# Attention exponentials split by PSUM bank, and value loads moved ahead of query and key loads

## The reference

```python
scores = jnp.einsum('bhqd,bhkd->bhqk', q, k) * SCALE
scores = jnp.where(causal, scores, -jnp.inf)
probs = jax.nn.softmax(scores, axis=-1)
out = jnp.einsum('bhqk,bhkd->bhqd', probs, v)
```

## Time and profile before

| | |
|---|---|
| median of 3 runs | 702.61 us (697.5 to 704.05) |
| the profiled execution | 697.29 us, span 695.6 us |
| mean granted TensorE clock | 0.932 of full speed |
| busy share of the span | PE 87%, PEld 73%, DVE 71%, ACT 51%, POOL 48% |
| chain that ended last, by engine | PE 42%, DVE 5%, POOL 5%, issue 5%, DMA 3%, ACT 3% |
| costliest attention line on ACT | L370, 48 calls, 49.1 us |

### The profile page before, as it was taken

The page is one execution under the profiler, slowest core; times in us unless marked ns, Lnnn a source line. Parts: engine busy times, 40 slices in busy tenths (PEclk is TensorE's granted clock), DMA queues, the critical chain, the costliest instruction groups (busy, mean ns, idle before and its releaser), DMA issues.

```text
span 695.6 us, 11909 instructions
## 1 busy us (share of the span) xinstructions
PE 603.9 (87%) x4100; PEld 504.4 (73%) x4100; DVE 497.2 (71%) x1066; ACT 352.9 (51%) x685; POOL 334.5 (48%) x322
## 2 busy tenths in 40 slices
PE   3787998998989789899998616999999999999992
PEld 2566887787876545466564416999999999999991
DVE  6887687788698857578883632778787888788740
ACT  4674563663553233353534213565666666656551
POOL 1065424324240014222543673446786868686776
PEclk9897999999999999899998655999999999999997
DMA  8411315775349756765745106233626262521224
GB/s 266 135 32 39 113 31 151 257 191 150 94 93 234 164 122 159 198 148 147 200 131 169 39 14 228 70 101 80 168 33 179 27 179 31 172 31 14 26 33 45
DMA packets 63317, 81.65 MB, mean 117 GB/s; under 512 B 10296, under 2 KB 47939, under 8 KB 63257
## 3 DMA queue, kind: packets, MB, share of 16 engines
q1 hardware_dynamic: 53928, 72.85, 37.4%
q0 software_dynamic: 9216, 7.81, 7.8%
q10 hardware_dynamic: 112, 0.23, 0.1%
HBM read 48.27 MB, written 34.36 MB: 119 GB/s over the span
## 4 chain that ended last, share of the span: by engine, by line
PE 42%; DVE 5%; POOL 5%; issue 5%; DMA 3%; ACT 3%; POOLq 0%; SPq 0%; ACTq 0%; DVEq 0%
PE l_scores L101 13%; PE l_turned L1899 7%; PE l_out L1899 3%; PE l_shared L1899 3%; PE l_turned L340 2%; POOL out L1603 2%; PE l_out L360 2%; PE l_turned L324 2%; POOL disp L1572 2%; PE l_scores L1833 2%; ACT l_area L370 2%; PE l_shared L1775 2%; PE l_scores L1856 1%; PE l_scores L265 1%; DMA l_hi<-vd 1%
## 5 line engine op out<-in xcount | busy, mean ns | idle before, releaser
L2088 DVE SCALAR_TENSOR_TENSOR w_v<-w_th,l_scores 128x324 f32<-128x324 f32 x128 | 62.2, 490 | 56.3 <-ACT w_th L1690 53.9
L1690 ACT ACTIVATE w_th<-l_scores 128x324 f32<-128x324 f32 x128 | 56.5, 441 | 84.0 <-PE l_scores L101 82.7
L1590 POOL TENSOR_TENSOR l_lo<-w_v,l_hi 128x324 fp32r<-128x324 f32 x64 | 59.0, 922 | 74.9 <-ACT l_hi L1696 74.7
L370 ACT ACTIVATE l_area<-l_turned 128x1024 f32<-128x1024 f32 x48 | 49.1, 1023 | 80.5 <-PE l_turned L340 77.4
L101 PE MATMUL l_scores<-l_hi,w_w1h 128*128 128x324 f32 x256 | 81.3, 318 | 2.3 <-DVE l_lo L2080 1.2
L1603 POOL DMA_INDIRECT out<-l_area,w_to x48 | 76.3, 1591 | 12.1 <-issue 9.7
L101 PE MATMUL l_scores<-l_lo,w_w1h 128*128 128x324 f32 x256 | 80.7, 315 | 0.0
L101 PE MATMUL l_scores<-l_hi,w_w1l 128*128 128x324 f32 x256 | 80.6, 315 | 0.0
L294 DVE TENSOR_REDUCE l_nm<-l_scores 128x4 f32<-128x1024 f32 (+1 forms) x45 | 54.7, 1216 | 22.0 <-PE l_scores L280 21.8
L1696 ACT ACTIVATE l_hi<-w_v 128x324 fp32r<-128x324 f32 x128 | 59.9, 472 | 12.4 <-DVE w_v L2088 11.8
L2062 DVE TENSOR_TENSOR w_w2l<-w_s,w_w2h 128x256 fp32r<-128x256 f32 x56 | 60.2, 1075 | 1.9
(11 more groups left out here) (459 smaller groups left out, 1704.1 us busy)
## 6 DMA issues: line engine op xcount, KB each, us to landing
w_s<-in_L_ffn_w SPq DMA_DIRECT2D x14, 1024.0 KB, 7.6
disp<-c_blank SPq DMA_DIRECT2D x8, 658.1 KB
l_lo<-kd SPq DMA_DIRECT2D x26, 200.0 KB
l_hi<-qd SPq DMA_DIRECT2D x26, 192.0 KB
w_rows<-disp SPq DMA_DIRECT2D x7, 658.1 KB
kd<-l_qkh SPq DMA_DIRECT2D x16, 256.0 KB, 4.7
vd<-l_area SPq DMA_DIRECT2D x4, 1024.0 KB, 6.5
qd<-l_qkh SPq DMA_DIRECT2D x16, 256.0 KB, 4.2
```

What stands on the lines that cost most here:

```text
L370: act.activation(lead.pr[n % 3][:, :], lead.tbank[:, :], ACT.Exp, scale=SCALE).then_inc(A["exp"], 1)
L1590: pool.tensor_tensor(hl[:, g % 3, half(1)], v[:, n % 4, :], hh[:, g % 3, half(1)].bitcast(F32), ALU.subtract)\
L1690: act.activation(th[:, n % 2, :], hb[n % 2][:, 0:HALF], ACT.Tanh, scale=0.5).then_inc(F["th"], 1)
L2088: dve.scalar_tensor_tensor(v[:, n % 4, :], th[:, n % 2, :], 1.0, hb[n % 2][:, 0:HALF], ALU.add, ALU.mult).then_inc(F["v"], 1)
```

## The change

There are two edits.

One: the exponentials of a step are made by two ACT calls of 512 columns, one per PSUM bank, and each counts on its own. So `turned` and `turned_mask` take the bank e as an argument, `st` and `exp` count twice per step, and the waits on them are doubled. In the second block PE now issues: mask of bank 0, products of bank 0, the `mask` matmuls of step t + 6, mask of bank 1, products of bank 1. In the first block: mask 0, products 0, mask 1, products 1.

Two: in SP's queue `load_values` stands right after `store_maxima`, ahead of `lay`, the query stores and the weight loads of that group.

```diff
-    ge(sp, A["st"], 3 * (g - ITEMS + 1))
+    ge(sp, A["st"], 6 * (g - ITEMS + 1))
...
+def turned_mask(pe, A, c, lead, n, e):
+
+    ge(pe, A["exp"], 2 * n + e - 1)
     if n == 0:
         pe.wait_ge(A["nm"], LEAD)
...
+    bank = lead.tbank[:, e * 4 * P:(e + 1) * 4 * P]
+    m = 4 if n % 3 == 2 else 2
...
+def turned(pe, A, lead, n, e):
 
     g, s = divmod(n, 3)
-    if s == 0:
+    if s == 0 and e == 0:
         pe.wait_ge(A[f"m_in{g % 2}"], 32 * (g // 2 + 1))
...
-    for p, e in heads(s):
-        rows = slice(64 * e, 64 * e + 3 * HD + 2)
...
+    rows = slice(64 * e, 64 * e + 3 * HD + 2)
...
+    for p in range(4):
+        if s == 2 or p // 2 == s:
+            at = e * 4 * P + (p if s == 2 else p % 2) * w
+            mm = pe.matmul(lead.tbank[:, at:at + w], kx[rows, p, key], q[rows, p, tok], start=False, stop=True,
+                           skip_group_check=True)
     mm.then_inc(A["st"], 1)
...
-    pe.wait_ge(A["exp"], n + 1)
+    pe.wait_ge(A["exp"], 2 * n + 2)
...
-    act.wait_ge(A["st"], n + 1)
     ge(act, A["pv"], n - 2)
-    act.activation(lead.pr[n % 3][:, :], lead.tbank[:, :], ACT.Exp, scale=SCALE).then_inc(A["exp"], 1)
+    for e in range(2):
+        act.wait_ge(A["st"], 2 * n + e + 1)
+        bank = slice(e * 4 * P, (e + 1) * 4 * P)
+        act.activation(lead.pr[n % 3][:, bank], lead.tbank[:, bank], ACT.Exp, scale=SCALE).then_inc(A["exp"], 1)
...
                     store_maxima(sp, A, lead, md, g)
+                    if g % 2 == 0 and g >= 4:
+                        load_values(sp, A, M, lead, vd, g // 2)
                     if 5 < g + 3 < GR:
                         lay(sp, A, M, lead, qd, kd, g + 3)
...
-                    if g % 2 == 0 and g >= 4:
-                        load_values(sp, A, M, lead, vd, g // 2)
...
                     if t < NS:
-                        turned_mask(pe, A, c, lead, t)
+                        turned_mask(pe, A, c, lead, t, 0)
+                        turned(pe, A, lead, t, 0)
                     if u < NS:
                         mask(pe, A, c, lead, u)
                     if t < NS:
-                        turned(pe, A, lead, t)
+                        turned_mask(pe, A, c, lead, t, 1)
+                        turned(pe, A, lead, t, 1)
```

More of the change, by code:

```diff
@@ L307, in turn_maxima @@
     dve.transpose(lead.mt[g % 2][:, :], mx[:, :, :].rearrange("q n c -> q (n c)").bitcast(F32)).then_inc(A["mx"], 1)
[L310 to L317, removed]
+def turned_mask(pe, A, c, lead, n, e):
+    ge(pe, A["exp"], 2 * n + e - 1)
     if n == 0:
         pe.wait_ge(A["nm"], LEAD)
[L320 to L328, removed]
+    bank = lead.tbank[:, e * 4 * P:(e + 1) * 4 * P]
+    m = 4 if n % 3 == 2 else 2
+    out = bank.rearrange("k (p q) -> k p q", p=m)[:, :, 0:P]
+    pe.matmul(out, c["mask"][:, :], c["identb"][:, :].unsqueeze(1).to_broadcast([P, m, P]),
+              start=True, stop=False, skip_group_check=True)
+def turned(pe, A, lead, n, e):
     g, s = divmod(n, 3)
-    if s == 0:
+    if s == 0 and e == 0:
         pe.wait_ge(A[f"m_in{g % 2}"], 32 * (g // 2 + 1))
     q, kx = lead.q3[g % ITEMS], lead.k3[g % ITEMS]
-    for p, e in heads(s):
-        rows = slice(64 * e, 64 * e + 3 * HD + 2)
[L336 to L341, removed]
+    rows = slice(64 * e, 64 * e + 3 * HD + 2)
+    tok = slice(P, L) if s == 2 else slice(0, L)
+    key = slice(P, L) if s == 2 else slice(0, P)
+    w = P if s == 2 else L
+    for p in range(4):
[3 more added lines that the diff above has]
+                           skip_group_check=True)
     mm.then_inc(A["st"], 1)
@@ L990, in step @@
                 def step(t):
-                    turned_mask(pe, A, c, lead, t)
-                    turned(pe, A, lead, t)
+                    for e in range(2):
+                        turned_mask(pe, A, c, lead, t, e)
+                        turned(pe, A, lead, t, e)
                 turn_x(0)
```

## The result

| kernel | median | executions | ratio to the kernel before, 95% interval |
|---|---|---|---|
| before | 701.80 us | 697.5 to 704.05, 5 | |
| changed | 749.93 us | 749.39 to 763.2, 5 | 1.0706 [1.0628, 1.0785] |

The change makes the kernel 7% slower. I had forecast slower, at 712 us, with 722 as the upper end. The five executions of the changed kernel lie at 749.4 to 749.9 us (three) and at 761.9 to 763.2 us (two), and the profiled one, 763.2 us, is one of the slower two; where sums are made, experiment 2 stands in for it, which has the same order on PE and whose profiled execution (750.65 us, span 748.9) agrees with the medians.

What follows compares the result with a forecast made beforehand. PE was taken to bound the attention, with small waits for ACT. Terms +23.8 - 5.0 - 2.3 - 3.4 - 1.0 = +12.1 on the profiled 697.29 us gave 709.4, predicted as 712 for a median of new runs; range 696 to 722.

Steps and rivals of the forecast that it cites:

- +.50 and +.70 per step: PE's attention steps: lost pairs and two more switches lengthen 256-column steps .76 to 1.26 us, 128-column steps 1.12 to 1.82.
- 20.4 us for steps 4 to 39: PE's added work in the attention to 361 us: 24 x .50 + 12 x .70 = 20.4 us.
- -3.4: About seven us at clock .51 after PE's stall for values, counted at full clock without the stall: -3.4 us.
- Steps 0 to 3, 40 to 45 and the rest: PE's added work: 2.2 us in 0 to 3, 0 in 40 to 43, 1.2 in 44 and 45, last two steps 0.
- +7.3 us hidden: ACT's two exponential calls instead of one: +.15 us per step, 7.3 over 48, hidden in ACT's idle time.
- The 5.0 us of waits: PE's waits for exponentials in the attention, 3.5 us shown, taken as 5.0 us gained.
- -2.3: PE's wait for the values of batch 2, until 282.86 us, goes when their load is issued earlier: -2.3 us.
- The 1.0 us for DVE: One wait of PE for DVE in the attention, absorbed by slower PE steps: -1.0 us.
- 1: PE's attention steps 4 to 39: PE's queue hides the added work, only gains stay, 686 to 691 us; chance .10.
- 2: PE's attention steps: only the loss of pairs is paid, 11.6 against 11.7 us gained, 697 to 703 us; chance .24.
- 3: Values' load: the 2.3 us reappear at group 5's maxima and the clock falls anyway; 715, up to 720; chance .12.
- rival 4: Products in one row half load their weights in the open, 9 us more, 718 to 724 us; chance .09.

Runs made afterwards that it cites:

- experiment 2: Kernel before with only PE's new order of masks and products; one exponential call per step, values' load not moved: 752.86 us, ratio 1.0698.
- experiment 9: Kernel before with odd heads' products in `turned` reading the even heads' rows, so no pairs and no added switch: 723.03 us, ratio 1.0298.
- experiment 5: Kernel before with pairs kept, but half of them ahead of the `mask` pair and half behind it: 718.08 us, ratio 1.0239.
- experiment 10: Changed kernel with the products of `turned` taken over all 128 rows: 707.13 us, ratio 1.0080.
- experiment 4: Kernel before with all products of bank 0 issued ahead of those of bank 1, in one place: 699.38 us, ratio 0.9969.
- experiment 3: Kernel before with two counted exponential calls after the last product, each turned mask waiting for one; pairs kept: 700.64 us, ratio 1.0005.
- experiment 1: Kernel before with only the `load_values` line moved as in the change: 699.97 us, ratio 0.9950.
- experiment 7: Kernel before with two counted exponential calls, pairs kept in one place, and the values' load moved ahead: 696.20 us, ratio 0.9942.
- experiment 11: Changed kernel with the second mask of a step waiting for the first bank's exponentials of the same step: 775.62 us, ratio 1.1068.
- experiment 12: Changed kernel with each mask of the turned bank issued four times in a row: 774.31 us.

## Why the prediction was wrong

**The step that failed: every step was priced at full clock.** I wrote +.50 and +.70 per step and summed 20.4 us for steps 4 to 39 from rows at full clock, and I gave the clock one term, -3.4, as something that PE loses after a stall and gets back without one. No rival had a long stretch of lower clock in which PE is busy. The runs show that term: 21 to 24 us in steps 4 to 39 (experiment 2, an estimate), against a miss of 750 - 712 = 38. The clock stays at the half level for 17 to 31 us at a time while PE is shown busy, when the products of a step share one half of the rows (experiment 9, once) or are cut by more switches (experiment 5); with both, as in the change, the loss is larger than the two together (18 + 22 us against 52 in experiment 2); with products over all rows the low stretches are 14 us and less and nearly all of the loss is gone (experiment 10).

**The prices of a step were right.** 1.30 and 1.84 us against 1.26 and 1.82, and the estimate of some 20 us of added work in experiment 2 stands beside the sum of 20.4. The reason I gave was half right: the pairs are lost since masks stand between the halves, not because one half's products are issued in a row (experiment 4).

**Steps 0 to 3, 40 to 45 and the rest.** In experiment 2 its span is 748.9 - 695.6 = 53.3 longer, 43.5 of it in steps 4 to 39; 3.6 lie ahead of them, where I had 2.2, and 6.2 behind, where I had 1.2. Behind them the half level lasts 64.8 us (418.3 to 428.6 and 432.0 to 486.6) against 51.2 before (371.8 to 378.6 and 388.8 to 433.2), so there, too, the clock has a part.

**Edit one on ACT.** +7.3 us hidden: right (8.0 us, 57.1 busy against 49.1, with ACT idle for 134.1). The 5.0 us of waits did go, but experiment 3 shows them to be worth nothing alone: 1.0005 [0.9965, 1.0045].

**Edit two.** Of -2.3 - 3.4, alone 0 to 7 us came (experiment 1), which holds the sum of 5.7 but does not tell the two terms apart. No run shows the clock's 3.4: the profiled execution of experiment 1, the slowest of its ten, has 107.0 us at .94 for steps 4 to 39, no better than before. In the changed kernel the 2.3 us wait is gone, 2.1 us of waits for maxima are new, and that place, 263 to 294, is at .51. The 1.0 us for DVE went as costed.

**The rivals.** 1 and 2: every switch in the new steps is paid. 3: its mechanism is real, waits for maxima of 1.8 us in experiment 1, 3.8 in experiment 7 and 2.1 in the changed kernel, but small. 4: products in one half follow after .12 (experiment 9), so their loads are hidden. That speaks against the rule on weight loads that rival 4 took from the Trainium skill, for products of one half too.

**What stays open.** Whether it is the logits that bring the clock down and the output projection that brings it back, as the places in experiment 2 suggest; and whether it is the empty rows or the short gaps at a switch that keep it down, since lost pairs and switches each go with long low stretches. The Trainium skill, "TensorE: Matmul & The Clock Gate", section "A second HAM failure mode: psum-queue depth-cycling", tells of a kernel whose clock swings between its two levels because PE idles briefly and often between groups of matmuls. Experiment 5 fits it (.83 with more switches). Experiment 11 does not bear it out: with pauses of up to .4 us the clock is .76, beside .75 without. Experiment 9, with no added gap and .50 over 27 us, is not covered by it.

## What to carry to other kernels

Price a reordering of TensorE's work at both levels of the clock: where a stage already lies close to PE's limit, ask what share of the array's rows the new order keeps in use, and give "the clock stays down for most of the stage" a rival with its own price, from steps read at both levels (here 1.5 to 1.6 times as long at the half level). Look also for where the clock goes down and comes back in the stage: here low stretches began at short waits and at a row of tiny matmuls, and their length went with the order. Keep matmuls of complementary row halves next to each other, without a full-row matmul between them; splitting them to release a consumer earlier pays only if the wait for that consumer sets the time. Waits of a few hundred nanoseconds in front of a saturated engine are worth nothing until a run shows otherwise.

## What the runs showed of the hardware

PE brings matmuls of different row halves together by itself, across instructions of other lines. In the timeline of the changed kernel the first product of `scores` (L280) starts at 295.19, ahead of the second product of `turned` (L335) at 295.41, although all of `turned` is issued first. The Trainium skill, "TensorE: Matmul & The Clock Gate", Part 3 (Packing small matmuls), says that matmuls start strictly in order; this trace shows otherwise.

A stage can run at half clock with PE shown busy throughout: 23.00 of 23 us at .50 (changed kernel, 349 to 372). Busy time alone doesn't show it; the clock's column does. And added matmuls can be mostly free there: 42 us of full-row masks cost 12 to 13 (experiment 12).
